# Turning the input of gate and up by transposing transfers for two of four batches

## The chip, the cores and the metric

The kernel runs on one core of one Trainium2 chip. The metric is the device time of one execution in microseconds (us). The core has five engines that run their own instruction queues and wait for each other through semaphores: TensorE (PE; its weight loads are shown as PEld), VectorE (DVE), ScalarE (ACT), GpSimd (POOL) and SyncE (SP), which here does nothing but start transfers. Each engine takes its instructions strictly in the order in which the program lists them.

## The reference

Four batches of 512 tokens, width 512, in single precision. Cut to what matters:

```python
x = _layernorm(x + attention(x, Wqkv, bqkv, Wo, bo))        # 16 heads
x = _layernorm(x + wkv(w, u, k=x, v=ctx))                   # a scan over the tokens
g = einsum('bsh,ih->bsi', x, (gate_w - 128) * gate_scale)   # 2048 wide
u = einsum('bsh,ih->bsi', x, (up_w - 128) * up_scale)
x = _layernorm(x + einsum('bsi,hi->bsh', silu(g) * u, (down_w - 128) * down_scale))
```

The second layernorm's output, called x2 below, is the input of gate and up. It stands in the tile `X[b]` with a token on each partition. The matmuls of gate and up sum over the 512 hidden columns, so they need x2 with a hidden column on each partition: it has to be turned.

## The kernel before

Numbers in single precision are multiplied as two 16-bit halves, a high one and a low one. For x2 these are `x2h` and `x2l`, each `[128, 2, 4, 512]`: 128 hidden columns, a slot of batch `b % 2`, four chunks c of hidden columns, 512 tokens.

The program's order is made by a timetable (`timetable()`): one list of pieces, with a slot counter, that every engine walks in the same order, each taking the pieces that are its own. Slots 0 to 275 are the attention of all four batches (16 head groups n of four heads, 16 slots a group). From slot 1000 (`FF`) on come gate, up and the down matmul, 20 slots a batch: 16 for the inner blocks `it`, then one for each `y(b, t)` (down, for 128 tokens t). Eight inner blocks of batch 0 (`EARLY`) are already spread over slots 246 to 276.

Turning x2 before the change, for each batch b and chunk c:

- piece `x2t`: PE transposes four 128x128 blocks of `X[b]` into one PSUM bank (`flip`, L1120, single precision);
- piece `x2h`: ACT reads the bank, scales by 64 and writes the high half in 16 bits (`x2_high`, L1359);
- piece `x2l`: DVE reads the bank again and writes what the high half lacks (`x2_low`, L1645).

`X2_AT` puts the four chunks of batch 0 at slots 222, 225, 226 and 233, and those of batch 1 all at slot 1018, which is after `y(0, 2)`. In the attention stage units like `x2t`, `wo`, `sv`, `pv` and `spread` share three PSUM banks. Batches 2 and 3 (`SEVEN`) use another scheme (`xf`, `xhi`, `xlo`) that the change leaves alone.

`gate_up` (L1133) waits for all of `x2h`, `x2l` of its batch. `y` is L1182 and L1184 (32 matmuls a piece). Around slot 1018 the list reads: `y(0, 1)`, `x1t(2, 2)`, `ek(2, 2)`, `scan_q(2, 2)`, `norm` and `out(0, 0)`, `scan_p`, `seed`, `refine(2, 2)`, `y(0, 2)` with its `yd`, `r3`, `rstd`, then `x2t(1, 0..3)`, `x1t(2, 3)`, `x2h` and `x2l` of batch 1, `ek(2, 3)`, `out(0, 1)`, further pieces of the scan, `y(0, 3)`, `gate(1, 0)`. `seed` (L1339, L1341) is an ACT piece of the scan and needs what POOL wrote at L1905.

SP starts, in this stretch of the attention, the transfers of `put` (L2057, the halves of q and k to memory), of `stack` (L2024, L2027, 128 KB each back into SBUF) and of `mput` (L2031 the shifts of a head group to memory, L2035 twice from there into `qs`); the transposed scores of group 14 (`turn`, L1056, first at slot 243) wait for the `mput(14)` at slot 238.

Of the kernel before, what the change touches and what calls it, by code (L numbers as in the profile page):

```python
# [5 lines left out]
ALU = mybir.AluOpType  # L6
ACT = mybir.ActivationFunctionType
# [5 lines left out]
P = 128  # L13
# [42 lines left out]
SEVEN = (2, 3)  # L56
PAIRS = IT // 2

SIGNAL = {"snap1": "snap", "snap5": "snap", "snap6": "snap", "c11": "summed", "c12": "summed", "c22": "summed"}

PART_READ = {1: 1, 2: 0, 3: 0, 4: 3, 5: 1, 6: 2, 7: 2}

# [29 lines left out]
            216, 15: 223}  # L92

WAIT = {'high': 1, 'low': 1, 'vtake': 2, 'r1': 2, 'norm': 6, 'exp': 4, 'eb': 0, 't1': 1, 't3': 0, 'oh': 2, 'ol':
        2, 'ek': 1, 'scan_q': 2, 'scan_p': 12, 'seed': 6, 'refine': 8, 'divide': 13, 'r2': 1, 'x2h': 0, 'x2l': 0,
        'expand': 0}
WAIT_IN = {'r1': 1, 'norm': 3, 'ek': 0, 'scan_q': 0, 'scan_p': 9, 'seed': 10, 'refine': 3, 'divide': 6, 'r2': 0,
           'x2h': 0, 'x2l': 0, 'norm2': 7}
PIECE_AT = {'load_second': 31, 'small': 66, 'split_wo': 47, 'load_ds': 180}
WU_AT = (44, 47, 48, 50)  # L100
WU_ZERO = (61, 119, 123, 144)
# [10 lines left out]
          3): 1040}  # L112
YT_AT = {0: (172, 178, 185, 191), 1: (1013, 1014, 1015, 1016), 2: (1026, 1027, 1028, 1029), 3: (1045, 1046, 1047,
         1049)}
X2_AT = {0: (222, 225, 226, 233), 1: (1018, 1018, 1018, 1018), 2: (1036, 1036, 1037, 1037), 3: (1057, 1057, 1057,
         1057)}
WO_IN = (7, 8, 9, 13)
WD_AT = (257, 257, 258, 261)
# [25 lines left out]
class Timetable:  # L144
# [45 lines left out]
def early(b, it):  # L190
# [11 lines left out]
    "bvo": lambda: ("bo",),  # L202
    "x1t": lambda b, c: ("ek", b, c),
    "yt": lambda b, t: ("r2", b, t),
    "x2t": lambda b, c: ("xf" if b in SEVEN else "x2l", b, c),
    "sa": lambda b, m: ("hfa", b, 2 * m + 1),
    "sb": lambda b, m: ("c11", b, m),
    "sd": lambda b, m: ("c12", b, m),
# [10 lines left out]
def timetable():  # L219
# [152 lines left out]

    def x2t(b, c):
        tt.flush(("norm", 1, b, 0, T))
        tt.unit("x2t", b, c)
        add("x2t", b, c)
        if b in SEVEN:
            late(wait("x2h"), lambda: quarters(b, c))
            return
        late(wait("x2h"), lambda: add("x2h", b, c))  # L380
        late(wait("x2l"), lambda: add("x2l", b, c))

    def quarters(b, c):
        add("xf", b, c)
# [8 lines left out]
    def gu_parts(b, it, pools):  # L393
        def part(p):
            name = "gate" if p < 2 else "up"
            if it == 0 and p == 0:
                tt.flush(("x2l", b, T - 1))
            if p % 2 == 0:
                tt.unit(name, b, it, pool=pools[p // 2])
                tt.unfinished.add((name, b, it))  # L400
            add(name, b, it, p % 2)
            if p % 2:
                tt.unfinished.discard((name, b, it))
            if p == 1:
                add("th", b, it)
                if early(b, it):
                    add("aa", b, it)
            if p == 3:
                add("hf", b, it)
# [287 lines left out]
def build(nc, ctx, xT, x, ctxT, wqkv, bqk, bv, wo, bo, wcol, ucol, gateT, gsc, upT, usc, downT, dsc,  # L697
# [47 lines left out]
    with ExitStack() as f:  # L745
# [10 lines left out]
        YS = sb(f, "ys", [P, 2, D], F32)  # L756
        S1A, S1B, S2B = (sb(f, n, [P, I], F16) for n in ("s1a", "s1b", "s2b"))
    CTS = [CT, CT, CT2, CT]
    RINGS = [(RING01[:, 0, :], RING01[:, 1, :]), (RING01[:, 2, :], RING01[:, 3, :]), (RING2[:, 0, :], RING2[:, 1, :])]


# [175 lines left out]
    def weight_sum(e, q, j, kk):  # L937
        a, c, op = {1: (wu[:, kk, :], wu[:, 2 + kk, :], ALU.add), 2: (WSUM[1][kk], wg[:, kk, :], ALU.subtract),
                    3: (wg[:, kk, :], wu[:, kk, :], ALU.subtract),
                    4: (wg[:, 2 + kk, :], WSUM[2][kk], ALU.subtract)}[j]  # L940
        q.wait_ge(*by("wo", B - 1, T - 1))
        if j == 4:
            q.wait_ge(sem("out0"), 16 * T)
        if j in (2, 4):
            q.wait_ge(*by_ws(j // 2, kk))
        e.tensor_tensor(WSUM[j][kk], a, c, op).then_inc(sem(f"ws{j}"), 1)
# [27 lines left out]
    def _(e):  # L974
# [148 lines left out]
        def gate_up(name, b, it, half):  # L1123
            bk, wt, s = bank[name, b, it], wg if name == "gate" else wu, b % 2
            if half == 0:
                emptied((name, b, it))
                pe.wait_ge(*by("x2h", b, T - 1))
                pe.wait_ge(*by("x2l", b, T - 1))
                pe.wait_ge(*by_zero("wg", T - 1))
                pe.wait_ge(*by_zero("wu", T - 1))  # L1130
            for k in (2 * half, 2 * half + 1):
                for xt in (x2h, x2l):
                    mm = e.matmul(PSB[:, bk, :], wt[:, k, it * P:(it + 1) * P], xt[:, s, k, :],  # L1133
                                  start=(k == 0 and xt is x2h), stop=(k == T - 1 and xt is x2l))
            if half:
                mm.then_inc(sem(name), 1)
# [104 lines left out]
    def _(e):  # L1241
# [104 lines left out]
            e.activation(X[b][:, t, :], X[b][:, t, :], ACT.Identity, bias=SHIFT[:, j:j + 1],  # L1346
                         scale=RS[:, 8 + b, t:t + 1]).then_inc(sem("norm2"), 1)

        def x2_high(b, c):
            act.wait_ge(*by("x2t", b, c))  # L1350
            if b >= 2:
                act.wait_ge(*by("up", b - 2, IT - 1))
            if b == 0:
                act.wait_ge(*by("qk", NG - 1, "k"))
                act.wait_ge(*by("v", B - 1, T - 1))
            elif b == 1:
                act.wait_ge(*by_put(NG - 1, "q"))
                act.wait_ge(*by_put(NG - 1, "k"))
            e.activation(x2h[:, b % 2, c, :], PSB[:, bank["x2t", b, c], :], ACT.Copy, scale=WS).then_inc(sem("x2h"), 1)  # L1359

        def x_full(b, c):
            act.wait_ge(*by("x2t", b, c))
# [143 lines left out]
    def _(e):  # L1506
# [132 lines left out]
            dve.wait_ge(sem(f"{name}_in{k * T // dst.shape[1]}"), 16)  # L1639
            e.tensor_scalar(dst[:, k, :], dst[:, k, :], -128.0, None, ALU.add).then_inc(sem("zero_" + name), 1)  # L1640

        def x2_low(b, c):
            s = b % 2
            dve.wait_ge(*by("x2h", b, c))
            e.scalar_tensor_tensor(out=x2l[:, s, c, :], in0=PSB[:, bank["x2t", b, c], :], scalar=WS, in1=x2h[:, s, c, :],  # L1645
                                   op0=ALU.mult, op1=ALU.subtract).then_inc(sem("x2l"), 1)

        def aa(b, it):
# [60 lines left out]
        def r3(b, t):  # L1709
            j = b * T + t  # L1710
            dve.wait_ge(*by("yd", b, t))
            dve.wait_ge(*by("x2t", b, T - 1))
            e.tensor_tensor(X[b][:, t, :], YS[:, j % 2, :], X[b][:, t, :], ALU.add).then_inc(sem("r3"), 1)
            stats(2, b, t, "r3")

# [15 lines left out]
        for name, *a in tt.order:  # L1731
# [8 lines left out]
                e.bn_aggr(MV[:, 2 * B + B - 1, T - 1, :], ST4[:]).then_inc(sem("ba2"), 1)  # L1740
            elif name == "scale_bqk":
                dve.wait_ge(sem("bqk"), 16)
                e.tensor_scalar(BQK[:], BQK[:], WS, None, ALU.mult).then_inc(sem("scale_bqk"), 1)
            elif name == "low":
                low(*a)
            elif name == "weigh":
# [11 lines left out]
            elif name == "bo":  # L1758
                dve.wait_ge(*by("bvo"))
                dve.wait_ge(*by_consts2())  # L1760
                e.tensor_tensor(BO[:], PSB[:, bank["bvo",], :], BO[:], ALU.add).then_inc(sem("bo"), 1)
            elif name == "split_wo":
                dve.wait_ge(sem("woh"), 1)
                dve.wait_ge(sem("warm"), 1)
# [235 lines left out]
    def _(e):  # L2000
# [37 lines left out]
        for name, *a in tt.order:  # L2038
# [11 lines left out]
            elif name == "load_w":  # L2050
                load_w(*a)
            elif name == "load_x":
                load_x(*a)
            elif name == "put":
                n, kind = a
                sp.wait_ge(*by("low", n, kind))
                e.dma_start(SCR[n, "qk".index(kind)].rearrange("l f t -> f l t"),  # L2057
                            HILO[kind][:]).then_inc(sem(f"put{kind}"), 16)
            elif name == "stack":
                stack(*a)  # L2060
            elif name == "mput":
# [86 lines left out]
```

## Time and profile before

| what | value |
|---|---|
| time, median of 3 runs | 710.17 us (708.37 to 712.4) |
| span of the profiled execution, first to last instruction | 709.9 us |
| busy: PE, DVE, ACT, POOL | 671.4, 513.2, 496.1, 395.7 us |
| mean clock granted to PE, of full speed | 0.989 |
| share of PE's pieces in the chain that ended last | 61% |

The profiled execution is one execution under the profiler. Its span lies 0.27 us below the median of the runs, inside their spread of 4 us. Every instruction has a start and a duration; where an engine stood idle before it, the trace names the instruction that ended the wait. A matmul's duration includes its passage through the array, so matmuls that follow each other overlap: what one costs in a row of many is the distance between their starts. "L1120" is a line of the kernel. The granted clock of PE is 1.00 at 2.4 GHz and 0.50 at 1.2 GHz.

### The profile page before, as it was taken

What the parts mean: (1) busy time and instruction counts of PE and PEld (TensorE: products, weight loads), DVE (VectorE), ACT (ScalarE), POOL (GpSimd) and SP (SyncE); (2) the same over time, 40 slices, a digit from 0 to 9 for tenths busy, and PEclk for the clock granted to TensorE, in tenths of its full rate; (3) what the DMA queues carried; (4) which work ended last, traced back from release to release, by engine and by line L of the source; (5) the groups of instructions that cost most, each with busy time, mean ns of one, the idle gap of its engine ahead of it and who ended that gap; (6) DMA issues with size and microseconds to landing.
All of it is one profiled execution on the core that took longest, in us unless ns stands there. A gap on an engine that the chain in (4) does not pass through costs nothing.

```text
span 709.9 us, 12525 instructions
## 1 busy us (share of the span) xinstructions
PE 671.4 (95%) x4290; PEld 380.8 (54%) x4290; DVE 513.2 (72%) x1220; ACT 496.1 (70%) x1143; POOL 395.7 (56%) x508
## 2 busy tenths in 40 slices
PE   8979999899988989799989999999999999999996
PEld 3435555445445545454445454544456797578845
DVE  4676767787888899989755569858777786655644
ACT  5798889789897879978787873384754855336620
POOL 6035735846999664864596654885771634103321
PEclk9999999999999999989999999999999999999999
DMA  7878944322332136460071002000001000000001
GB/s 239 249 218 235 217 145 135 98 75 79 124 102 78 38 85 163 120 143 16 8 120 60 1 0 75 16 31 0 1 1 44 17 1 2 30 31 1 1 16 45
DMA packets 45024, 54.33 MB, mean 77 GB/s; under 512 B 5921, under 2 KB 33825, under 8 KB 44961
## 3 DMA queue, kind: packets, MB, share of 16 engines
q1 hardware_dynamic: 41264, 46.85, 21.6%
q0 software_dynamic: 3264, 6.29, 5.4%
q8 instruction: 34, 0.56, 0.3%
q10 hardware_dynamic: 432, 0.39, 0.2%
q14 instruction: 30, 0.24, 0.1%
HBM read 45.00 MB, written 12.71 MB: 81 GB/s over the span
## 4 chain that ended last, share of the span: by engine, by line
PE 61%; DVE 13%; ACT 10%; POOL 5%; issue 5%; DMA 4%; SPq 1%; POOLq 0%; DVEq 0%; ACTq 0%
PE psb L1160 12%; PE psb L1133 8%; PE psb L996 6%; PE psb L1184 5%; PE psb L1182 5%; PE psb L1104 4%; PE psb L1072 4%; PE psb L1027 4%; DVE ee L1530 3%; PE psb L1039 3%; PE psb L1056 3%; DVE x L1607 2%; PE psb L1120 2%; PE psb L1083 2%; ACT L1330 1%
## 5 line engine op out<-in xcount | busy, mean ns | idle before, releaser
L1530 DVE CUSTOM_DVE_ANT_0 ee<-psb,mask,clip 128x512 f32<-128x512 f32 (+3 forms) x256 | 131.3, 542 | 24.9 <-PE psb L1039 22.3
L1278 ACT ACTIVATE ee<-ee,nm 128x512 f32<-128x512 f32 (+3 forms) x256 | 142.2, 560 | 1.4 <-DVE nm L1530 1.4
L1938 POOL TENSOR_TENSOR hl<-ring,hh 128x512 f16<-128x512 f32 x64 | 80.1, 1264 | 86.7 <-ACT hh L1414 57.3
L1288 ACT ACTIVATE ee<-psb 128x256 f32<-128x256 f32 (+1 forms) x192 | 94.6, 523 | 31.0 <-PE psb L1056 21.0
L1182 PE MATMUL psb<-wd,hh 128*128 128x512 f16 x240 | 91.0, 379 | 0.0
L1184 PE MATMUL psb<-wd,hl 128*128 128x512 f16 x240 | 91.0, 379 | 0.0
L1868 POOL TENSOR_SCALAR_AFFINE_SELECT ee<-ee 128x256 f32<-128x256 f32 x128 | 56.8, 452 | 60.7 <-ACT ee L1288 59.9
L1039 PE MATMUL psb<-ks,qs 128*128 128x512 f16 (+3 forms) x256 | 72.5, 305 | 8.3 <-DVE nm L1530 6.1
L1056 PE MATMUL psb<-qs,ks 128*128 128x128 f16 (+3 forms) x256 | 60.1, 306 | 9.6 <-ACT ee L1288 7.5
L996 PE MATMUL psb<-xh,wqk 128*128 128x512 f16 x240 | 61.8, 385 | 1.7 <-POOL xh L1830 1.2
L1885 POOL TENSOR_TENSOR rs<-ve,half 128x1 f32<-128x1 f32 (+1 forms) x24 | 20.5, 854 | 72.0 <-DVE ve L1599 71.7
L1278 ACT ACTIVATION_READ_ACCUMULATOR ee<-ee,nm 128x1 f32 x256 | 51.0, 199 | 0.0
L1133 PE MATMUL psb<-x2h,wg 128*128 128x512 f16 x128 | 48.6, 380 | 0.8 <-ACT ring L1426 0.5
L1133 PE MATMUL psb<-x2h,wu 128*128 128x512 f16 x128 | 48.5, 379 | 0.0
L1133 PE MATMUL psb<-x2l,wu 128*128 128x512 f16 x128 | 48.5, 379 | 0.0
L1133 PE MATMUL psb<-x2l,wg 128*128 128x512 f16 x128 | 48.5, 379 | 0.0
L1039 PEld LDWEIGHTS psb<-ks,qs 128*128 128x128 f16 x256 | 25.0, 99 | 35.6 <-DVE nm L1530 11.5
L1441 ACT ACTIVATE hh<-ring 128x512 bf16<-128x512 f32 x32 | 20.2, 630 | 30.6 <-DVE ring L1662 30.6
L1056 PEld LDWEIGHTS psb<-qs,ks 128*128 128x128 f16 x256 | 23.6, 99 | 32.1 <-ACT ee L1288 14.8
L1072 PE MATMUL psb<-ee,v 128*32 128x128 f32 (+3 forms) x512 | 37.8, 435 | 0.7 <-POOL ee L1868 0.6
L1184 PEld LDWEIGHTS psb<-wd,hl 128*128 128x128 f16 x240 | 23.4, 98 | 27.3 <-POOL hl L1938 0.2
L1182 PEld LDWEIGHTS psb<-wd,hh 128*128 128x128 bf16 x240 | 23.4, 98 | 27.2
(217 smaller groups left out, 1668.2 us busy)
## 6 DMA issues: line engine op xcount, KB each, us to landing
qs<-parts SPq DMA_DIRECT2D x48, 128.0 KB, 2.7
ks<-parts SPq DMA_DIRECT2D x45, 128.0 KB, 2.9
parts<-qhl SPq DMA_DIRECT2D x16, 256.0 KB, 2.2
parts<-khl SPq DMA_DIRECT2D x16, 256.0 KB, 2.2
x<-in_x SPq DMA_DIRECT2D x4, 1024.0 KB, 6.8
ct<-in_ctxT SPq DMA_DIRECT2D x4, 1024.0 KB, 5.1
out<-x SPq DMA_DIRECT2D x16, 256.0 KB, 2.0
xt<-in_xT SPq DMA_DIRECT2D x14, 256.0 KB, 3.4
```

Of the source, the lines that this page charges most:

```text
L996: mm = e.matmul(PSB[:, bk, :], wt[:, k, c0:c0 + P], xt[:, k, :], start=(p == 0 and k == 0), stop=(p == 2 and k == T - 1))
L1039: e.matmul(PSB[:, bank["score", H, i], 0:w], heads(n, "q")[:, h, i * P:(i + 1) * P], heads(n, "k")[:, h, 0:w], start=True, stop=True).then ...
L1056: mm = e.matmul(PSB[:, bk, o:o + (T - j) * P], heads(n, "k")[:, h, j * P:(j + 1) * P], heads(n, "q")[:, h, j * P:S], start=True, stop=True)
L1072: mm = e.matmul(PSB[32 * h:32 * h + 32, bk, j * P:S], VV[:, b % 2, j, g * P + 32 * h:g * P + 32 * h + 32], ET[(4 * n + h) % ET_SLOTS][:, T ...
L1133: mm = e.matmul(PSB[:, bk, :], wt[:, k, it * P:(it + 1) * P], xt[:, s, k, :], start=(k == 0 and xt is x2h), stop=(k == T - 1 and xt is x2l))
L1160: mm = e.matmul(PSB[:, bk, k * HALF_S:(k + 1) * HALF_S], weights(j, kk, 2 * m + k), moving(b, j, kk, low), start=(unit is not None and k + ...
L1182: e.matmul(PSB[:, bk, :], HS[it][0][:, t * P:(t + 1) * P], wd[:, it, :], start=(it == 0), stop=False)
L1184: mm = e.matmul(PSB[:, bk, :], HS[it][1][:, t * P:(t + 1) * P], wd[:, it, :], start=False, stop=(it == IT - 1))
L1278: e.activation(dst, dst, ACT.Exp, bias=NM[:, n % 4, col:col + 1], scale=-1.0, accum_out=DEN[:, n % 4, col:col + 1]).then_inc(sem("exp"), 1)
L1288: e.activation(ET[H % ET_SLOTS][:, base:base + width], PSB[:, bank["turn", H, item], 0:width], ACT.Exp, scale=SC).then_inc(sem("et"), 1)
L1530: e.tensor_tensor_reduce(E[H % E_SLOTS][:, EOFF[i]:EOFF[i] + w], PSB[:, bank["score", H, i], 0:w], MASK[:, S - w:S], -SC, CLIP[:, i:i + 1] ...
L1938: e.tensor_tensor(HS[it][1][:], pair(b, it // 2)[:, it % 2, :] if b in SEVEN else ring(b, it)[1], HS[it][0][:], ALU.subtract).then_inc(sem ...
```

## The change

For batches 0 and 1 the three pieces change their order: first the split, by token, then the turn, by transfers.

- `x2h`: ACT reads `X[b][:, t, :]` (SBUF, tokens t) and writes the high half into a staging tile `STAGED[b][0]`, still with a token on each partition. `x2l`: DVE does the same for the low half, from SBUF too.
- `xtr`, new, on SP: for each t, two transposing transfers of `[128 tokens, 512]` in 16 bits (128 KB each), from the staging tiles into `x2h` and `x2l`. That is 8 a batch, 16 in all. Each set waits for its `x2l`.
- `x2t` is gone for these batches: 8 pieces, 32 PE transposes.
- Batch 0 stages in the slot of batch 1 of `x2h`, `x2l`; batch 1 stages in `S1B`, `S2B`, which are weight sums of the later scheme, so `weight_sum` with j 1 or 2 and kk 1 now waits for batch 1's transfers. The staging tile of batch 0 overlaps the halves of q and k, so `x2l` of batch 0 waits for `put(15)`.
- `X2_AT[0]` moves from (222, 225, 226, 233) to (231, 231, 232, 232). Batch 1 stays at slot 1018.
- `gate_up` waits for the transfers (`by_turned_x2`). `r3` waits for `x2h` where it waited for `x2t`. Two semaphores of other pieces (`scale_bqk`, `bo`) become one.

```diff
-X2_AT = {0: (222, 225, 226, 233), 1: (1018, 1018, 1018, 1018), ...
+X2_AT = {0: (231, 231, 232, 232), 1: (1018, 1018, 1018, 1018), ...
...
     def x2t(b, c):
         tt.flush(("norm", 1, b, 0, T))
+        if b not in SEVEN:
+            for name in ("x2h", "x2l", "xtr"):
+                add(name, b, c)
+            return
...
+    STAGED = [(x2h[:, 1, :, :], x2l[:, 1, :, :]), tuple(w[:].rearrange("p (t n) -> p t n", t=T) for w in (S1B, S2B))]
...
+    def by_turned_x2(b):
+        return sem("xtr"), 2 * 16 * T * (b + 1)
...
+        if j in (1, 2) and kk == 1:
+            q.wait_ge(*by_turned_x2(1))
...
-                pe.wait_ge(*by("x2h", b, T - 1))
-                pe.wait_ge(*by("x2l", b, T - 1))
+                pe.wait_ge(*by_turned_x2(b))
...
-        def x2_high(b, c):
-            act.wait_ge(*by("x2t", b, c))
...
+        def x2_high(b, t):
+            act.wait_ge(*by_norm(1, b, t))
+            if b:
+                act.wait_ge(*by("wo", B - 1, T - 1))
+            else:
                 act.wait_ge(*by("qk", NG - 1, "k"))
                 act.wait_ge(*by("v", B - 1, T - 1))
...
-            e.activation(x2h[:, b % 2, c, :], PSB[:, bank["x2t", b, c], :], ACT.Copy, scale=WS).then_inc(sem("x2h"), 1)
+            e.activation(STAGED[b][0][:, t, :], X[b][:, t, :], ACT.Copy, scale=WS).then_inc(sem("x2h"), 1)
...
+        def x2_low(b, t):
+            dve.wait_ge(*by("x2h", b, t))
+            if b == 0:
+                dve.wait_ge(*by_put(NG - 1, "q"))
+                dve.wait_ge(*by_put(NG - 1, "k"))
+            e.scalar_tensor_tensor(out=STAGED[b][1][:, t, :], in0=X[b][:, t, :], scalar=WS, in1=STAGED[b][0][:, t, :],
                                    op0=ALU.mult, op1=ALU.subtract).then_inc(sem("x2l"), 1)
...
+            elif name == "xtr":
+                b, t = a
+                sp.wait_ge(*by("x2l", b, t))
+                if b:
+                    sp.wait_ge(*by_turned_x2(b - 1))
+                for k, to in enumerate((x2h, x2l)):
+                    e.dma_start_transpose(to[:, b, :, t * P:(t + 1) * P], STAGED[b][k][:, t, :]).then_inc(sem("xtr"), 16)
```

## Rows read from the trace of the kernel before

**Rows 1.** Busy time of the engines in stretches (first line: the columns).
```profile
core 0: us, PE busy (x) PEld busy (x) DVE busy (x) ACT busy (x) POOL busy (x), PEclk, DMA share, GB/s
320.00:330.00 10.00, 9.56 (x73) 4.97 (x66) 9.41 (x28) 8.26 (x27) 4.56 (x9) 1.00 0.01 3
455.00:520.00 65.00, 64.32 (x310) 30.46 (x309) 46.70 (x59) 41.47 (x57) 47.28 (x39) 1.00 0.03 13
```

**Rows 2.** Timeline, PE, batch 0's transposes: start, us, engine, line, tiles, count.
```profile
308.30 0.86 PE L1120 MATMUL psb<-ident,x 128*128 128x128 f32 x4
309.00 0.22 PE L1039 MATMUL psb<-ks,qs 128*128 128x128 f16 x1
...
312.59 0.60 PE L1120 MATMUL psb<-ident,x 128*128 128x128 f32 x4
313.03 0.27 PE L1039 MATMUL psb<-ks,qs 128*128 128x256 f16 x1
```

**Rows 3.** Timeline, 305 to 314 us: waits around batch 0's first chunk.
```profile
309.83 0.69 DVE L1645 SCALAR_TENSOR_TENSOR x2l<-psb,x2h 128x512 f16<-128x512 f32 x1 [2.32 <-ACT x2h L1359]
310.57 1.16 PE L1083 MATMUL psb<-lt,v 128*128 128x128 f32 x8 [0.26 <-DVE x2l L1645]
```

**Rows 4.** Timeline, DVE, where slots 231 and 232 fall.
```profile
320.31 0.35 DVE L1530 CUSTOM_DVE_ANT_0 ee<-psb,mask,clip 128x128 f32<-128x128 f32 x1
322.71 0.74 DVE L1530 CUSTOM_DVE_ANT_0 ee<-psb,mask,clip 128x512 f32<-128x512 f32 x1
```

**Rows 5.** Timeline, SP and PE: the shifts of group 14 and their first reader.
```profile
328.47 0.31 SPq L2031 DMA_DIRECT2D shifts<-mrow  x1
329.84 0.78 SPq L2035 DMA_DIRECT2D qs<-shifts  x2
332.76 0.49 PE L1056 MATMUL psb<-qs,ks 128*128 128x512 f16 x2
```

**Rows 6.** Timeline around slot 1018, all engines.
```profile
445.88 2.32 PEld L1120 LDWEIGHTS psb<-ident,x 128*128 128x128 f32 x20
448.17 0.10 PEld L1182 LDWEIGHTS psb<-wd,hh 128*128 128x128 bf16 x1
...
450.90 0.63 ACT L1339 ACTIVATE qs_<-ek 128x512 f32<-128x512 f32 x1 [9.55 <-POOL ek L1905]
452.11 2.04 ACT L1359 ACTIVATE x2h<-psb 128x512 f16<-128x512 f32 x4
452.72 2.48 DVE L1645 SCALAR_TENSOR_TENSOR x2l<-psb,x2h 128x512 f16<-128x512 f32 x4 [1.83 <-ACT x2h L1359]
...
455.35 0.38 PE L1133 MATMUL psb<-x2h,wg 128*128 128x512 f16 x1
```

**Rows 7.** Lines of SP: ns to issue one (min/median/max), and us to landing.
```profile
L2027 SPq DMA_DIRECT2D ks<-parts x45: 303/432/1152, 24.5 to 315.2; - x45
...
DMA to landing us min/median/max: 2.4/2.8/7.6
...
L2035 SPq DMA_DIRECT2D qs<-shifts x32: 302/372/1726, 38.2 to 352.5; - x32
...
DMA to landing us min/median/max: 2.1/2.2/4.4
...
L2049 SPq DMA_DIRECT2D ident<-in_cmask x1: 2146/2146/2146, 5.8 to 5.8; - x1
```

**Rows 8.** Stretches before and at a fall of PE's clock (columns as in Rows 1).
```profile
298.40:301.00 2.60, 0.40 (x3) 0.10 (x1) 2.60 (x4) 2.38 (x7) 1.36 (x2) 1.00 1.04 170
302.00:308.80 6.80, 6.10 (x19) 2.47 (x17) 5.28 (x13) 3.75 (x10) 6.70 (x9) 0.50 0.26 68
216.70:220.10 3.40, 3.40 (x16) 2.88 (x15) 2.04 (x10) 2.78 (x9) 3.25 (x5) 0.50 0.14 46
```

**Rows 9.** By line and shape, whole span: the low half from PSUM, and one from SBUF.
```profile
L1645 DVE SCALAR_TENSOR_TENSOR x2l<-psb,x2h 128x512 f16<-128x512 f32 x8 | 5.2, 685 | 4.6 <-ACT x2h L1359 4.6
L1766 DVE SCALAR_TENSOR_TENSOR wol<-ct,woh 128x512 f16<-128x512 f32 x4 | 2.5, 694 | 1.5 <-ACT woh L1476 1.5
```

More of the change, by code:

```diff
@@ L57 @@
 PAIRS = IT // 2
-SIGNAL = {"snap1": "snap", "snap5": "snap", "snap6": "snap", "c11": "summed", "c12": "summed", "c22": "summed"}
+SIGNAL = {"snap1": "snap", "snap5": "snap", "snap6": "snap", "c11": "summed", "c12": "summed", "c22": "summed", "scale_bqk": "biases", "bo": "biases"}
 PART_READ = {1: 1, 2: 0, 3: 0, 4: 3, 5: 1, 6: 2, 7: 2}
@@ L94 @@
 WAIT = {'high': 1, 'low': 1, 'vtake': 2, 'r1': 2, 'norm': 6, 'exp': 4, 'eb': 0, 't1': 1, 't3': 0, 'oh': 2, 'ol':
-        2, 'ek': 1, 'scan_q': 2, 'scan_p': 12, 'seed': 6, 'refine': 8, 'divide': 13, 'r2': 1, 'x2h': 0, 'x2l': 0,
+        2, 'ek': 1, 'scan_q': 2, 'scan_p': 12, 'seed': 6, 'refine': 8, 'divide': 13, 'r2': 1, 'x2h': 0,
         'expand': 0}
 WAIT_IN = {'r1': 1, 'norm': 3, 'ek': 0, 'scan_q': 0, 'scan_p': 9, 'seed': 10, 'refine': 3, 'divide': 6, 'r2': 0,
-           'x2h': 0, 'x2l': 0, 'norm2': 7}
+           'x2h': 0, 'norm2': 7}
 PIECE_AT = {'load_second': 31, 'small': 66, 'split_wo': 47, 'load_ds': 180}
@@ L114 @@
          1049)}
-X2_AT = {0: (222, 225, 226, 233), 1: (1018, 1018, 1018, 1018), 2: (1036, 1036, 1037, 1037), 3: (1057, 1057, 1057,
+X2_AT = {0: (231, 231, 232, 232), 1: (1018, 1018, 1018, 1018), 2: (1036, 1036, 1037, 1037), 3: (1057, 1057, 1057,
          1057)}
@@ L204 @@
     "yt": lambda b, t: ("r2", b, t),
-    "x2t": lambda b, c: ("xf" if b in SEVEN else "x2l", b, c),
+    "x2t": lambda b, c: ("xf", b, c),
     "sa": lambda b, m: ("hfa", b, 2 * m + 1),
@@ L374, in x2t @@
         tt.flush(("norm", 1, b, 0, T))
+        if b not in SEVEN:
+            for name in ("x2h", "x2l", "xtr"):
+                add(name, b, c)
+            return
         tt.unit("x2t", b, c)
         add("x2t", b, c)
[L377 to L381, printed above, removed]
+        late(wait("x2h"), lambda: quarters(b, c))
     def quarters(b, c):
@@ L396, in part @@
             if it == 0 and p == 0:
-                tt.flush(("x2l", b, T - 1))
+                tt.flush(("xtr", b, T - 1))
             if p % 2 == 0:
@@ L1347, in out_norm @@
                          scale=RS[:, 8 + b, t:t + 1]).then_inc(sem("norm2"), 1)
-        def x2_high(b, c):
-            act.wait_ge(*by("x2t", b, c))
-            if b >= 2:
-                act.wait_ge(*by("up", b - 2, IT - 1))
-            if b == 0:
+        def x2_high(b, t):
[3 more added lines that the diff above has]
+            else:
                 act.wait_ge(*by("qk", NG - 1, "k"))
                 act.wait_ge(*by("v", B - 1, T - 1))
-            elif b == 1:
-                act.wait_ge(*by_put(NG - 1, "q"))
-                act.wait_ge(*by_put(NG - 1, "k"))
-            e.activation(x2h[:, b % 2, c, :], PSB[:, bank["x2t", b, c], :], ACT.Copy, scale=WS).then_inc(sem("x2h"), 1)
+            e.activation(STAGED[b][0][:, t, :], X[b][:, t, :], ACT.Copy, scale=WS).then_inc(sem("x2h"), 1)
         def x_full(b, c):
@@ L1640, in zero @@
             e.tensor_scalar(dst[:, k, :], dst[:, k, :], -128.0, None, ALU.add).then_inc(sem("zero_" + name), 1)
[L1642 to L1645, printed above, removed]
+        def x2_low(b, t):
[4 more added lines that the diff above has]
+            e.scalar_tensor_tensor(out=STAGED[b][1][:, t, :], in0=X[b][:, t, :], scalar=WS, in1=STAGED[b][0][:, t, :],
                                    op0=ALU.mult, op1=ALU.subtract).then_inc(sem("x2l"), 1)
@@ L1711, in r3 @@
             dve.wait_ge(*by("yd", b, t))
-            dve.wait_ge(*by("x2t", b, T - 1))
+            dve.wait_ge(*by("x2t" if b in SEVEN else "x2h", b, T - 1))
             e.tensor_tensor(X[b][:, t, :], YS[:, j % 2, :], X[b][:, t, :], ALU.add).then_inc(sem("r3"), 1)
@@ L1742, in _ @@
                 dve.wait_ge(sem("bqk"), 16)
-                e.tensor_scalar(BQK[:], BQK[:], WS, None, ALU.mult).then_inc(sem("scale_bqk"), 1)
+                e.tensor_scalar(BQK[:], BQK[:], WS, None, ALU.mult).then_inc(sem("biases"), 1)
             elif name == "low":
@@ L1760, in _ @@
                 dve.wait_ge(*by_consts2())
-                e.tensor_tensor(BO[:], PSB[:, bank["bvo",], :], BO[:], ALU.add).then_inc(sem("bo"), 1)
+                e.tensor_tensor(BO[:], PSB[:, bank["bvo",], :], BO[:], ALU.add).then_inc(sem("biases"), 1)
             elif name == "split_wo":
```

## The prediction

> **What bounds the kernel now.** I read the busy time of the engines by stretches first [rows 1]. Behind the attention PE is the bound: 64.32 of 65.0 us, no other engine over 47.3. What PE loses there is lost for good; what it is spared is gained only if nothing else is late. In the attention two engines are close: of 10 us around slot 231 PE is busy 9.56 and DVE 9.41. The change meets both kinds of stretch: batch 0 in the attention, batch 1 at the seam between the down matmul of batch 0 and gate and up of batch 1. So I read the timelines of those two places next, engine by engine, and asked of each: which wait ends last before the first matmul that reads x2?
>
> At the seam the answer is plain [rows 6]. PE ends `y(0, 2)`, does 20 transposes in 2.32 us (16 of batch 1's x2, 4 for the scan), then `y(0, 3)` from 448.17, and the first gate matmul of batch 1 starts at 455.35. The last of the four `x2l` ends at 452.72 + 2.48 = 455.20. So the gate starts as soon as `x2l` is there: the seam has no slack at all. Nor is `x2l` late because of PE's transposes. ACT sat idle for 9.55 us until POOL's L1905 let the scan's `seed` go at 450.90, and `x2h` stands behind that `seed` in ACT's queue, so it began at 452.11, four microseconds after its banks were full. The change leaves `seed` ahead of `x2h`: both are added where they were.
>
> **Part 1, PE is spared 32 transposes.** In batch 0 a chunk of four costs the distance to the next start: 0.70 us for the first, which ran at the low clock, and 0.44 for the second [rows 2]; the other two cost about as much as the second, so 0.70 + 3 x 0.44 = 2.0 us. With them goes a wait of PE for the bank, 0.26, and one of DVE for `x2h`, 2.32 [rows 3]. DVE is nearly as full as PE, so its idle time counts too, but it lies beside PE's 0.70 of the same chunk and isn't added twice. I take 2.0 + 0.3 = 2.3 us gained, with ends 0 (DVE remains the bound) and 2.8. In batch 1 PE is spared 2.32 x 16/20 = 1.86 us, but that gains nothing, since `x2l` is what the gate waits for: `y(0, 3)` now ends at about 453.3 in the clock of before, and PE waits.
>
> **Part 2, the split from SBUF.** Eight pieces on ACT and eight on DVE as before, with another source. DVE's `x2l` from PSUM takes 685 ns, the same operation from SBUF (L1766) 694 [rows 9]. ACT's I leave at the 2.04 us that four took [rows 6]. Nothing, either way. Four `x2l` now stand in two slots instead of four; the 2.8 us of DVE work is the same, only bunched, and PE has matmuls of the out projection to go on with. Nothing, at most 0.7 (one `x2l` in front of a score that PE waits for).
>
> **Part 3, batch 1's turn.** This is new work on the path that sets the end. From each `x2l` on: two transfers to issue by SP, in order, then the landing of the eighth, then the gate. Nothing else of SP stands in the way; behind it waits only an output that nobody reads on the chip. The DMA engines are idle (share 0.03 on average after 455) [rows 1].
>
> The trace of before holds no transposing transfer. Its cost is bounded by the nearest rows [rows 7]. Lower end: `ks<-parts`, 128 KB into SBUF by the same queue, takes SP 0.43 us to issue (median). Upper end: the longest issue I found, 2.15. Landing after issue begins: 2.4 to 7.6 us, median 2.8. I take 1.0 us for an issue, near the longest that a transfer of this very size took (1.15), because eight follow each other and each is cut finer than one that keeps its rows; and 2.8 for landing.
>
> The first `x2l` ends at 452.72 + 0.69 = 453.4. The eighth issue begins 7 x 1.0 later, at 460.4, and lands at 463.2. Against 455.35 the gate is late by **7.9 us**. With 0.43 and 2.4 it would be 458.8, late by 3.5; with 2.15 and 2.8 it would be 471.3, late by 15.9.
>
> **Part 4, PE's clock.** PE then stands idle from 453.3 to 463.2. In the trace a stretch of 2.60 us in which PE worked 0.40 was followed by 6.8 us at 1.2 GHz; another fall lasted 3.4 us [rows 8]. Half the length is lost while PE has work: 1.7 to 3.4 us. I take **1.7**, with 0 as the lower end, since a fall may pass while PE is idle anyway.
>
> **Part 5, batch 0's turn.** DVE comes to `x2l` of slot 231 behind the score at 320.31, so the first ends at about 321.4 and the second at 322.0; the other two stand behind the score at 322.71 and end near 325.5 and 326.2 [rows 4]. At 1.0 us an issue SP is done with eight at about 329.5. The gate of batch 0 comes at slot 246, some ten slots after that, so its own wait is covered. What isn't, is SP's queue: `mput(14)` is next in it. Before, it was issued at 328.47, the second of its two reads was begun at 330.2 (329.84 and one issue of 0.37) and landed 2.2 us later, at 332.4, and the transposed score that reads it started at 332.76 [rows 5, 7]. The cover is 0.35 us. SP would come to it 1.0 us later: PE loses **0.7**. At 0.43 an issue: nothing. At 2.15: eight end at 338.6, ten late, PE loses 9.8.
>
> **Part 6, the rest.** The merged semaphore counts the same two pieces in the same order; `r3` waits for a piece long done; `weight_sum`'s new wait falls some blocks into gate and up of batch 1, tens of microseconds after the eighth landing, in front of nothing that PE wants at once. POOL's queue is not touched. All nothing.
>
> **The sum.** +7.9 + 1.7 + 0.7 - 2.3 = +8.0 us against the profiled execution (span 709.9). The median of the runs is 0.3 above that span, within their spread, so I add to it: 710.2 + 8.0 = **718.2 us**, 1.1% slower.
>
> **Rivals.** (A) *An issue costs what any other of its size costs.* Place: SP's queue at the seam; price 3.5 to 3.9 late, minus 2.3, plus 0 to 1.7: +1.2 to +3.3, 712.4 in the middle, which is no change by the measure. For it speaks that every 128 KB row lies near 0.43; against it, that no row turns anything. It decides below 0.47 us an issue, where the sum -1.95 + 7 x issue + 2.8 + 1.7 - 2.3 falls under 3.55 us (0.5%). It can't well become faster: with no fall of the clock and 2.8 gained it is still +0.7, as two transfers must come after an `x2l` that was itself just in time.
> The Trainium skill (Advanced Engine Details and Errata, section X-Bar Transpose (TRN2)) has the rule that speaks for A: transposing transfers are as fast as regular ones. No row of before shows one; by that rule 712.4.
>
> (C) *They are served one after the other, each when the last has landed.* Eight times 2.8 is 22.4: the gate at 475.8, late by 20.4, plus a fall of 3.4, minus 2.3: +21.5, 732. If the shifts of group 14 stand behind batch 0's eight in the same rings (321.4 + 22.4 = 343.8, plus the 3.9 that they take, against 332.76) PE loses another 15: 747. Against it: an ordinary transfer's issue of 0.43 beside a landing of 2.8 [rows 7] means that several are under way at once.
> PE's own price is 2.32/20 = 0.12 us a square in a row of twenty [rows 6]. The Trainium skill (VectorE: DVE Perf Modes, section The three transpose paths) speaks against the change here: 1309 ns for one 128x128 square by the DMA crossbar, 390 by TensorE; the row has TensorE at a third of that, and the crossbar in no row. By the Trainium skill's figure four squares take 5.2 us and eight transfers 42, an estimate of some +40 us.
>
> **How the numbers follow.** Forecast (issue 0.6 to 1.3 us): 50%, own range 712 to 726 (0.6: 460.0, +4.7, no fall, -2.8; 1.3: 465.3, +10.0, +3.4, -1, +3.0 for the shifts). Rival A: 26%, 710.5 to 713.5. Rival C: 14%, 732 to 747. Between forecast and C: 5%. Faster for a reason that I don't see, such as the fall of 6.8 us at 302 being gone in most runs together with A: 5%. The range **710.5 to 731** leaves out C, and the faster cases: about 2 in 10. A measurement of this kernel tells 0.5% (3.6 us) from no change: faster 0.05, same 0.28 (A and the lower edge of the forecast), slower 0.67.
>
> **What would show it.** In the changed kernel's timeline: `x2h` of batch 1 still right behind the scan's `seed` on ACT; a gap on PE behind `y(0, 3)` that ends with the transposing transfers, of 5 (A), 10 (forecast) or over 20 us (C); a granted clock of 0.50 right after it; SP's rows of the new line show the issue (0.43, 1.0 or more) and the landing; `mput(14)` issued after the eighth. Wrong would be: no gap of PE there, `x2h` of batch 1 well ahead of `seed`, or PE waiting longest in the attention instead.

## The result: 1.7% slower

| | before | after |
|---|---|---|
| time, median of 4 runs each | 711.28 us (708.37 to 713.31) | 721.84 us (720.86 to 724.86) |
| ratio, 95% interval | | 1.0174, 1.0132 to 1.0216 |
| span of the profiled execution | 709.9 us | 720.9 us |

The waits of PE over the whole span of after name the two places at once. The columns are: who waited for what, us in total, times, longest.

```profile
PE psb L1138 <- DMA x2l<-s2b: 12.1, 1, 12.1
...
PE psb L1062 <- DMA qs<-shifts: 3.4, 2, 2.9
```

The first is the seam, where L1138 is the gate of batch 1; the second is the transposed score of group 14. Next the timeline of the seam in after, which answers to [rows 6].

```profile
451.28 0.63 ACT L1344 ACTIVATE qs_<-ek 128x512 f32<-128x512 f32 x1 [9.56 <-POOL ek L1909]
...
452.48 2.17 ACT L1361 ACTIVATE s1b<-x 128x512 f16<-128x512 f32 x4
...
453.13 3.87 DVE L1649 SCALAR_TENSOR_TENSOR s2b<-x,s1b 128x512 f16<-128x512 f32 x4 [1.87 <-ACT s1b L1361]
...
454.32 1.20 SPq L2095 DMA_TRANSPOSE x2h<-s1b  x1
455.56 1.27 SPq L2095 DMA_TRANSPOSE x2l<-s2b  x1
...
463.41 1.27 SPq L2095 DMA_TRANSPOSE x2l<-s2b  x1
...
466.04 0.59 PE L1138 MATMUL psb<-x2h,wg 128*128 128x512 f16 x1 [12.07 <-DMA x2l<-s2b]
```

`seed` (L1344) still waits for POOL and `x2h` stands right behind it. Eight issues follow each other without a pause, 1.24 us from the first to the second and 1.31 between most of the others (454.32 to 463.41 is 9.09 us for 7 distances), and PE stands idle for 12.07 us. The issues and the landing by line (ns to issue, shortest, median, longest; then us from issue to landing):

```profile
L2095 SPq DMA_TRANSPOSE x2h<-s1b x4: 1196/1264/1265, 454.3 to 462.1; - x4
L2095 SPq DMA_TRANSPOSE x2l<-s2b x4: 1267/1267/1267, 455.6 to 463.4; - x4
...
DMA to landing us min/median/max: 2.4/2.5/4.2
```

Stretches of after, columns as in [rows 1]: the gap, and the fall of the clock that begins in it and ends 3.1 us after the gate has started.

```profile
453.70:466.00 12.30, 0.27 (x2) 0.00 (x0) 11.73 (x13) 6.06 (x9) 10.72 (x10) 0.71 0.44 91
459.00:469.30 10.30, 3.26 (x9) 1.23 (x10) 7.12 (x8) 3.25 (x4) 7.00 (x7) 0.51 0.45 116
```

Two traces are compared here by the start of the same matmul in each. The clock falls elsewhere too, and not at the same places in each execution (before: 6.8 us at 302, [rows 8]; after: none there), so a shift is read only across the stretch in question, and even there a fall in one of the two traces has to be taken out. Up to `y(0, 2)` after is 0.37 us behind before. The gate of batch 1 starts 10.69 us behind (455.35 and 466.04), so the seam costs **10.32**. Eight matmuls at half clock add 1.51 (12.20). Between 480 and 486 us 1.25 of that is regained, where before had small waits of its own: after is then 10.95 behind, and stays so to the end.

Batch 0, timeline of SP, ACT and PE in after, which answers to [rows 5]:

```profile
317.85 2.21 SPq L2095 DMA_TRANSPOSE x2h<-x2h  x1
...
327.96 1.27 SPq L2095 DMA_TRANSPOSE x2l<-x2l  x1
329.28 0.58 SPq L2035 DMA_DIRECT2D shifts<-mrow  x1
330.90 0.77 SPq L2039 DMA_DIRECT2D qs<-shifts  x2
...
325.40 0.27 ACT L1300 ACTIVATE mrow<-psb 32x128 f16<-32x128 f32 x1
...
333.50 0.27 PE L1062 MATMUL psb<-qs,ks 128*128 128x256 f16 x1 [2.88 <-DMA qs<-shifts]
```

The rows to be moved are there at 325.67, but the shifts (L2035) are issued at 329.28, behind the eighth transfer.

### The profile page after: what moved, and what is told of

The parts are those of the page before. It is cut to its first block, busy times and chain, and to the rows that moved or that the text cites. A ratio compares the mean times of both kernels' runs of the same rounds, so it can differ in the third digit from the quotient of the medians.

```text
span 720.9 us, 12476 instructions
## 1 busy us (share of the span) xinstructions
PE 667.5 (93%) x4258; PEld 377.7 (52%) x4258; DVE 516.3 (72%) x1220; ACT 497.6 (69%) x1143; POOL 396.1 (55%) x508
## 4 chain that ended last, share of the span: by engine, by line
PE 61%; DVE 12%; ACT 9%; DMA 5%; issue 5%; POOL 4%; SPq 3%; POOLq 0%; DVEq 0%; ACTq 0%
PE psb L1165 12%; PE psb L1138 12%; PE psb L1002 5%; PE psb L1187 5%; PE psb L1189 5%; PE psb L1033 4%; PE psb L1110 4%; PE psb L1078 4%; DVE ee L1532 3%; PE psb L1062 3%; PE psb L1045 3%; DVE x L1609 2%; SPq L2095 2%; PE psb L1126 2%; ACT ee L1283 2%
## 5 line engine op out<-in xcount | busy, mean ns | idle before, releaser
L1138 PE MATMUL psb<-x2h,wg 128*128 128x512 f16 x128 | 49.5, 387 | 12.2 <-DMA x2l<-s2b 12.1
L1138 PE MATMUL psb<-x2l,wg 128*128 128x512 f16 x128 | 49.4, 386 | 0.0
L1138 PE MATMUL psb<-x2h,wu 128*128 128x512 f16 x128 | 48.5, 379 | 0.0
L1138 PE MATMUL psb<-x2l,wu 128*128 128x512 f16 x128 | 48.5, 379 | 0.0
L1666 DVE SCALAR_TENSOR_TENSOR ring<-ring,c,psb 128x512 f32<-128x512 f32 x24 | 17.9, 747 | 33.8 <-ACT ring L1428 22.3
```

## The experiments

Theory T: nearly all of the loss is batch 1's turn at the seam, the issues of SP behind a late `x2l`; batch 0 comes out about even. Its rivals: batch 0 carries much of it (R1), or any transfer there costs as much, turned or not (R2). Each time is set against executions of before on the same chip. The table gives what the traces say about the seam, worked out as above: when the gate of batch 1 starts, how far the kernel is from before ahead of the seam, and what the seam has cost by the start of the gate and by the last down matmul.

| kernel | gate (1, 0) | ahead | cost at the gate | cost at the end |
|---|---|---|---|---|
| after | 466.04 | +0.37 | +10.32 | +10.58 |
| batch 0 alone | 455.28 | -0.09 | +0.03 | +0.02 |
| batch 1 alone | 464.09 | -1.70 | +10.44 | +11.64 |
| shifts first | 461.34 | -4.35 | +10.34 | +10.47 |
| plain copies | 460.29 | -1.09 | +6.03 | +6.16 |
| split early | 462.33 | +5.04 | +1.95 | +2.39 |
| half turned | 466.75 | +1.39 | +10.02 | +11.61 |
| filler | 466.99 | +0.90 | +10.74 | +9.50 |
| joined | 459.45 | -2.08 | +6.18 | +6.41 |
| joined, early | 450.66 | -2.77 | -1.92 | +1.95 |

The last two columns differ by the fall of the clock behind the gap less what is regained later. The fall is not the same in each execution: 1.51 us in after, 2.44 in batch 1 alone, 2.83 in half turned; regained are 1.24 or 1.25 in all three. A gate "in the clock of after" below is the gate less the "ahead" of its own row, plus 0.37.

**One batch at a time.** The edit: `b in (0,)` or `b in (1,)` takes the new path, the other batch keeps `x2t`, `x2h`, `x2l` at the old slots.

> Only batch 0 is split and turned by transfers; batch 1 goes over PE as before. Theory T (the loss is batch 1's turn at the seam, eight issues of 1.3 us in SP's queue behind x2l): what PE is spared in batch 0 (2.3 us) and what it loses in waiting for the shifts of group 14 (about 2.9) cancel, so 0 to +1 us against before, about 711 to 712; the seam is as before, the first gate matmul of batch 1 right behind the fourth x2l. Rival R1 (batch 0 carries a good part, by the shifts' wait and the bunched x2l): +4 us or more.

> Only batch 1 is split and turned by transfers; batch 0 goes over PE at its old slots. Theory T: about +10.5 us, about 721.8, as after; the PE gap behind y(0, 3) ends with the transposing transfers and is as long as in after, followed by the clock at 0.50. Rival R1 (batch 0 carries a good part): +7 us or less.

Measured: batch 0 alone 711.92 against 710.06 us, ratio 1.0022 (0.9997 to 1.0048). Batch 1 alone 720.70, ratio 1.0153 (1.0100 to 1.0206), +10.6 us. The gate of batch 1 in batch 0 alone, then in batch 1 alone:

```profile
455.28 0.38 PE L1145 MATMUL psb<-x2h,wg 128*128 128x512 f16 x1
```
```profile
464.09 0.58 PE L1147 MATMUL psb<-x2h,wg 128*128 128x512 f16 x1 [12.20 <-DMA x2l<-s2b]
```

R1 falls. Batch 0 alone is near the upper edge of what T said, or a little over it.

Since both kernels have the same seam or the same batch 0 as after, batch 0's own parts can be read off too. Against batch 1 alone, the transposed scores of after shift by -2.40 us between 298 and 322 us (-2.42 in batch 0 alone), by +1.04 from there to 326 us, and by +2.44 at the shifts of group 14: +1.08 in all.

The -2.40 has three parts. Batch 1 alone ran 3.4 us at half clock here, where after and batch 0 alone had no fall (a stretch of batch 1 alone, columns as in [rows 1]):

```profile
301.50:305.30 3.80, 3.38 (x10) 1.04 (x9) 3.73 (x8) 3.10 (x8) 3.72 (x6) 0.55 0.23 73
```

That is 0.57 us of the shift, and none of it comes from the change. PE's transposes and its wait for the bank are 2.27. Against them stands a wait that grew by 0.44 at the first score behind the bunched split (batch 1 alone, then after):

```profile
322.02 0.28 PE L1067 MATMUL psb<-qs,ks 128*128 128x256 f16 x1 [0.25 <-ACT ee L1302]
```
```profile
320.62 0.28 PE L1062 MATMUL psb<-qs,ks 128*128 128x256 f16 x1 [0.69 <-ACT ee L1293]
```

So the change gains 2.27 here and loses 0.44 + 1.04 = 1.48 around the split.

**The shifts first.** Two of batch 0's four pieces `xtr` are listed behind `mput(14)`:

```diff
     def shifts(n):
         ...
         add("mput", n)
+        if n == NG - 2:
+            add("xtr", 0, 2)
+            add("xtr", 0, 3)
```

> Both batches by transfers, but four of batch 0's eight transposing transfers stand behind the shifts of group 14 in SP's list instead of ahead of them. Theory T: the wait of 2.9 us of the transposed score on qs<-shifts falls under 0.5, and the time by 2 to 3 us against after, to about 719; the gate of batch 0, some ten slots later, doesn't wait for the transfers. Rival (DVE is as full as PE there, so PE's wait only moves to DVE's tiles): the wait falls, and the time stays at that of after, 721.8.

SP's timeline in that kernel, and PE's wait over its whole span:

```profile
320.62 1.28 SPq L2100 DMA_TRANSPOSE x2l<-x2l  x1
324.01 0.33 SPq L2040 DMA_DIRECT2D shifts<-mrow  x1
```
```profile
PE psb L1067 <- DMA qs<-shifts: 1.0, 1, 1.0
```

The shifts go out at once, and of the wait 1.0 us is left in the whole span, none of it between 315 and 334. From 298 us to batch 0's gate this kernel loses nothing against batch 1 alone but gains 1.90, where after loses 1.08: a gain of 3.0 in that stretch, and none of it is the clock's, since this kernel had a fall there and after had none. Its time doesn't show it: 721.39 us (717.78 to 724.23), ratio 1.0161 (1.0107 to 1.0214), too wide to tell it from after. The kernels with batch 0 alone, below, tell it better.

**Plain copies.** `dma_start` in place of `dma_start_transpose`, the same pieces and bytes.

> All sixteen transposing transfers are ordinary transfers of the same pieces; left out is the turn itself, so x2h and x2l of batches 0 and 1 hold tokens where hidden columns should be. Theory T (the turning form costs 1.27 us of SP's time an issue, an ordinary transfer of this size 0.43): SP keeps up with x2l, the gate of batch 1 starts at the last x2l (457.0 in the clock of after) + 0.4 + 2.4, about 460 against 466, and the time is 715 to 716. Rival R2 (a transfer as such is what costs, turned or not): the gate at about 466 as in after, 721 to 722.

Measured 715.60 us, ratio 1.0073 (1.0047 to 1.0099). R2 falls as it was put, though more than half of the loss at the gate, 6.03 of 10.32 us, stays. By line, and the gate:

```profile
L2095 SPq DMA_DIRECT2D x2h<-s1b x4: 594/623/654, 452.9 to 457.1; - x4
L2095 SPq DMA_DIRECT2D x2l<-s2b x4: 639/644/650, 453.5 to 457.8; - x4
...
DMA to landing us min/median/max: 2.3/2.4/4.0
```
```profile
460.29 0.58 PE L1138 MATMUL psb<-x2h,wg 128*128 128x512 f16 x1 [7.78 <-DMA x2l<-s2b]
```

So 4.3 of the 10.3 us (10.32 - 6.03) are the turning form, nearly all of it in the issue: 1.27 us against 0.64, and 4.89 from the first issue to the eighth against 9.09. Landing is the same. The other 6.0 are 0.55 by which the first transfer goes out later than the first `x2l` ended in before, these 4.89, and 2.53 to the gate, less the 1.94 that before itself has from its first `x2l` to the gate. An issue of 0.43, which T took from [rows 7], isn't reached with these pieces either, and SP did not keep up with `x2l`. T's 460 was meant in the clock of after, where this gate comes at 461.75, 1.7 later; that it stands at 460.29 in its own trace is chance.

**Split early.** `X2_AT[1]` is 1017 in place of 1018, so `x2h` stands ahead of `seed` on ACT; the last piece that subtracts 128 from the down weights (`ZERO_IN`) moves one slot earlier with it.

> As after, with batch 1's split and turn one slot earlier (1017 in place of 1018), so that its x2h stands ahead of the scan's seed on ACT and not behind it. Theory T (the loss is what lies between a late x2l and the gate, and x2l is late because of the place behind seed): x2l begins right behind the second layernorm of batch 1, near 443.5 us in the clock of after, eight issues of 1.31 us end near 455, the gate comes at 457 to 458 instead of 466, eight us earlier, the clock falls less, and the time is 712 to 715. Rival (the scan behind x2h and x2l becomes late in their place and gives the gain back): the gate comes early, but the time stays above 718.

Measured 714.77 us, ratio 1.0067 (1.0041 to 1.0092). The profiled execution was the slowest of the eight.

```profile
449.92 2.49 DVE L1649 SCALAR_TENSOR_TENSOR s2b<-x,s1b 128x512 f16<-128x512 f32 x4
```
```profile
462.33 0.49 PE L1138 MATMUL psb<-x2h,wg 128*128 128x512 f16 x1 [3.70 <-DMA x2l<-s2b]
```

The seam costs 1.95 in place of 10.32: the place of the split is worth 8.4 us. In the clock of after the gate comes at 457.7, as expected. The four `x2l` take 2.49 again.

**Half turned.** Batch 1's transfers turn two chunks of four.

```diff
+n = T // (1 + b)
...
-e.dma_start_transpose(to[:, b, :, t * P:(t + 1) * P], STAGED[b][k][:, t, :]).then_inc(sem("xtr"), 16)
+e.dma_start_transpose(to[:, b, 0:n, t * P:(t + 1) * P], STAGED[b][k][:, t, 0:n * P]).then_inc(sem("xtr"), 16)
```

> Batch 1's eight transposing transfers turn two of the four chunks each (64 KB in place of 128 KB); left out is the turn of chunks 2 and 3 of batch 1, so those parts of x2h and x2l hold old numbers. If the price goes by the 128x128 squares, an issue takes 0.6 to 0.8 us in place of 1.27 and the gate comes 2.5 to 4 us earlier than in after (from 466.0, to 462 or 463), limited by x2l, whose fourth ends at 457. If it goes by the transfer, the issue stays at 1.2 to 1.3 us and the gate at 466.

```profile
L2096 SPq DMA_TRANSPOSE x2h<-s1b x4: 1175/1244/1244, 455.3 to 463.0; - x4
L2096 SPq DMA_TRANSPOSE x2l<-s2b x4: 1246/1247/1247, 456.5 to 464.3; - x4
...
DMA to landing us min/median/max: 2.3/2.4/5.3
```

Half the bytes, the same issue (1.25) and a seam of +10.02. From 64 to 128 KB the price goes by the transfer. This is read from the trace; the kernel ran once, in 724.68 us.

**Filler.** PE does 56 spare matmuls ahead of the gate's wait.

```diff
+if (name, b, it) == ("gate", 1, 0):
+    for _ in range(FILL):   # 56
+        e.matmul(PSB[:, bk, :], wd[:, 0, 0:P], wd[:, 1, :], start=True, stop=True)
```

> As after, with 56 more matmuls of 128x512 on loaded weights between y(0, 3) and the gate of batch 1 on PE, into the bank that the gate then overwrites: some 12 us of work that fills the gap. Theory T (PE's idle gap makes the clock fall, and that costs 1.5 us of its own): no stretch at 0.50 behind the gap, the gate at the same time as in after, and the time 1 to 2 us below after's, near 720. Rival (the fall costs nothing, since PE waits for others later anyway): no stretch at 0.50 either, but later waits of PE grow by the same and the time stays at 721 to 722.

```profile
466.99 0.39 PE L1142 MATMUL psb<-x2h,wg 128*128 128x512 f16 x1 [0.40 <-DMA x2l<-s2b]
467.21 0.38 PE L1142 MATMUL psb<-x2l,wg 128*128 128x512 f16 x1
```

The gate's matmuls follow at 0.22 us, the granted clock has no stretch at 0.50 there, and the seam costs 9.50 by the end in place of 10.58. The rival, that later waits grow by as much, falls in the trace: 1.24 is regained later, as in after. So the fall costs 1.5 us, of which 1.1 shows at the end, because the gate came 0.4 later here; the first issue took 1.99 us in place of 1.20:

```profile
454.57 1.99 SPq L2099 DMA_TRANSPOSE x2h<-s1b  x1
```

The runs, 722.20 us and 1.0167 (1.0133 to 1.0200), can't tell 1 us; the trace bears T out, the time leaves it open.

**Joined.** High and low half of 128 tokens lie side by side in one staging tile and one tile `X2`, and are turned by one transfer of 256 KB: four in place of eight for batch 1.

```diff
+e.dma_start_transpose(X2[:, b, :, :, t * P:(t + 1) * P].rearrange("p j c n -> p (j c) n"),
+                      JOINED[:, t, :, :].rearrange("p j n -> p (j n)")).then_inc(sem("xtr"), 16)
```

> As after, with batch 1's transfers joined: the high and the low half of 128 tokens stand side by side in the staging tile and are turned by one transfer of 256 KB, so four transfers in place of eight, in the same place behind x2l, with the same bytes. If the price goes by the transfer (theory T after the run that turned half as much at the same 1.25 us an issue): issue 1.2 to 1.35 us each, SP keeps up with x2l, the fourth lands near 461 to 462 in place of 465.9 (clock of after), and the time is 3.5 to 5 us under after's, 717 to 718. If it goes by the bytes once they are above 128 KB: issue near 2.5 us each and the gate at 466, 721 to 722.

```profile
L2098 SPq DMA_TRANSPOSE x2both<-s x4: 1231/1282/1332, 451.9 to 456.0; - x4
...
DMA to landing us min/median/max: 3.1/3.2/3.4
```

Twice the bytes at the same issue, 0.7 us more to land. The seam costs 6.18, which is 4.1 less, and in the clock of after the gate comes at 461.9; both as expected. The time is 719.86 us (716.11 to 722.52), 1.0142 (1.0107 to 1.0177), lower than after but above what was expected; four scattered runs don't settle it to 2 us.

**Versions that might beat before.** Batch 0 alone with the shifts first, run twice; the same with its split in four slots in place of two; and batch 1 joined and early, with batch 0's shifts first.

> Only batch 0 by transfers, and four of its eight stand behind the shifts of group 14 in SP's list. Theory T (batch 0 gains what PE is spared, 2.3 us, less about 1.0 at the bunched x2l, once the shifts aren't behind the transfers): 0.7 to 2 us below before, ratio 0.997 to 0.999, and about 2.5 us below the kernel with batch 0 alone. Rival (DVE is the bound in that stretch and PE's spared time is not gained): the same as before or above it.

> The kernel with batch 0 alone and the shifts first once more, beside the spread one on the same chip: 708 to 709.5, ratio 0.996 to 0.999, if the gain seen first was no accident of the runs; 710 or above if it was.

> As the kernel with batch 0 alone and the shifts first, with batch 0's four pieces of the split in slots 230, 231, 232, 233 in place of two in 231 and two in 232. Theory T (the bunched x2l stand ahead of scores that PE's turned scores wait for; PE's waits there add up to about 1.5 us against 0.25 before): the step of +1.0 us between the shift of PE's turned scores at 318 and at 324 us halves or goes, and the time is 0.5 to 1 us under the bunched kernel, 707.5 to 708.5. Rival (DVE is as full as PE there, so the same 2.6 us of x2l cost the same wherever they stand): the step stays at 1.0, the time at 708.6.

> Batch 1's four joined transfers, its split one slot earlier (1017), and for batch 0 four of the eight transfers behind the shifts of group 14. Theory T: four issues of 1.3 us behind an x2l that ends some 6 us ahead of the end of y(0, 3) land before y(0, 3) ends, PE has no gap at the seam and gains the 1.86 us of transposes of batch 1, beside 1 to 2 us of batch 0: 3 to 4 us below before, 706 to 707, ratio 0.994 to 0.996. Rival (the place ahead of seed delays the scan of batch 2, and PE or DVE pay for it later): at 709 or above.

| kernel | time | before, same chip | ratio, 95% |
|---|---|---|---|
| batch 0, shifts first | 708.64 | 710.16 | 0.9970 (0.9946 to 0.9995) |
| the same again | 708.96 | 709.00 | 0.9988 (0.9964 to 1.0012) |
| batch 0, shifts first, split spread | 708.33 | 709.00 | 0.9978 (0.9956 to 0.9999) |
| batch 1 joined and early, shifts first | 710.09 | 710.24 | 1.0000 (0.9982 to 1.0018) |

Batch 0 with the shifts first gains 2.0 us in both traces, counted as above against batch 1 alone. Of this 0.6 is again the fall that only batch 1 alone had, so the change is worth 1.4; the intervals put it between no gain and 0.5%. Spreading the split gained 1.30 in its trace, not more, and the loss around the split is as large as with the bunched one (1.5 us in both): the theory that bunching causes it falls. What remains fits DVE being full there, 9.90 of the 10 us from 320 in after, where before had 9.41 [rows 1]; no run tests that by itself.

```profile
320.00:330.00 10.00, 8.58 (x48) 4.39 (x49) 9.90 (x32) 8.76 (x28) 5.93 (x13) 1.00 0.58 103
```

The last kernel, joined and early, is the one to learn from; its 706 to 707 us were missed, and the rival's 709 or more came. PE has no gap at the seam and gains 1.92 us there. Then it waits, and its clock falls (timeline, and a stretch with columns as in [rows 1]):

```profile
478.33 0.66 PE L1134 MATMUL psb<-ident,ct 128*128 128x128 f32 x4 [1.69 <-ACT ring L1436]
```
```profile
480.00:483.30 3.30, 3.30 (x10) 1.16 (x8) 2.41 (x3) 1.15 (x3) 1.35 (x2) 0.53 0.00 0
```

ACT's `ring` stands behind the next `seed` of the scan. It is 1.81 us earlier than in before (477.59 and 479.40) where PE is 4.69 earlier. From the start of the gate to the end 3.87 us are given back (-1.92 to +1.95 in the table). 2.88 of them go at this wait (-4.69 to -1.81): the 1.92 that PE had gained at the seam and the scan did not follow, and 0.96 by which the scan itself is late. The rest, 0.99, goes in the fall of the clock behind it, less what is regained. Split early tells where the 0.96 comes from, since it has the early split without the joined transfers. The first `seed` in split early, then here:

```profile
457.38 0.63 ACT L1344 ACTIVATE qs_<-ek 128x512 f32<-128x512 f32 x1 [7.13 <-POOL ek L1909]
```
```profile
449.58 0.63 ACT L1352 ACTIVATE qs_<-ek 128x512 f32<-128x512 f32 x1 [7.13 <-POOL ek L1917]
```

Against before's 450.90 [rows 6], and with what each kernel was ahead or behind taken out, that is 1.44 and 1.45 us late, and the `ring` is 0.95 and 0.96 late. With the split in its old place the same `seed` is within 0.03 of before, and 0.27 early in the filler's trace. So the early split does delay the scan.

## Why the prediction was right, and where its sizes were off

The sign, the place and the mechanism came out as forecast: `x2h` right behind `seed`, one gap of PE behind `y(0, 3)`, a low clock after it, `mput(14)` behind the eighth issue. The time, 721.84, lies inside the range and 3.6 us above the 718.2. That it came so near is in part luck: three terms were too small, all in the same direction, and 1.25 us regained later and a fall of the clock that after happened not to have hid some of it.

| term | forecast | measured |
|---|---|---|
| first `x2l` ends (first issue 454.32, less 0.37) | 453.4 | 453.9 |
| first to eighth issue | 7.0 | 9.1 |
| landing | 2.8 | 2.5 |
| gate of batch 1 late | 7.9 | 10.3 |
| half clock behind the gap | 1.7 | 1.5 |
| regained later | 0 | -1.25 |
| PE spared in batch 0 | -2.3 | -2.3 |
| half clock near 302 us, in batch 1 alone and not in after | - | -0.6 |
| split of batch 0 on DVE | 0 (to 0.7) | +1.5 |
| shifts of group 14 | 0.7 | +2.4 |
| sum | +8.0 | +11.7 |

The sum adds the gate and the six rows below it, before rounding. It stands beside 11.0 between the two spans, 10.6 between the two medians and +12.4 (9.4 to 15.4) from the ratio. The three larger misses:

- **Part 3, the issue.** It was put at 1.0 us between 0.43 and 2.15; it is 1.27, with 1.30 from one to the next on average. That is 2.1 us at the seam. The choice of a value above the plain transfers was right; the reason given, finer pieces, explains only 0.43 to 0.64, which plain copies of these pieces cost. The rest is the turning form, for which the prediction had no row, so that 1.0 came near 1.27 was luck.
- **Part 5, the shifts.** The same price: the prediction's own line said 3.0 at 1.3 us an issue. The 2.21 us of the first issue came on top. The step at the wait itself is 3.0; 0.6 of it is made up by waits of PE close by that were gone. The shifts first undid it.
- **Part 2, the split from SBUF.** "Nothing, either way" was wrong at both places. In batch 0 PE's waits for DVE and ACT grew. At the seam the price per piece was read from `wol` [rows 9], beside which POOL computed on nothing wider than 16 columns. Here four `x2l` took 3.87 us against 2.48 [rows 6]. Of this only the 0.5 by which the first one ends later is in the seam's 10.32: SP went from the first issue to the eighth without a pause, so that the fourth `x2l`, 1.4 later than in before, held up nothing.

Part 4 was right in size, but not that part of it would be regained. Part 1's 2.3 was right as a stretch, and the loss around the split, where DVE is nearly full, ate 1.5 of it.

Rival A said that an issue costs what any other costs. It does not: 1.27 against 0.43 [rows 7], and against 0.64 in plain copies of the same pieces. The rule of the Trainium skill (Advanced Engine Details and Errata, section X-Bar Transpose (TRN2)), that transposing transfers are as fast as regular ones, holds here for landing (2.5 and 2.4 us) and not for eight in a row. Rival C would have shown a distance of 2.8 from one issue to the next. The Trainium skill's 1309 ns for one 128x128 square (VectorE: DVE Perf Modes, section The three transpose paths) does not add up square by square here: 1.29, 1.31 and 1.27 to 1.38 us lie between whole transfers of two, four and eight squares, and no run turns one square alone. The eight transfers took 9.09 + 2.63 us from the first issue to the gate, where the prediction's estimate from that figure had 42.

## What to carry to other kernels

Work taken off a full engine is worth only what the replacement doesn't put on the path: here 1.9 us of transposes of batch 1 were traded for eight issues behind a split that was already just in time, and splitting earlier, with the same transfers, took away 8.4 of the 10.3 us. Read a transfer's price as issue times number plus one landing, ask what stands behind it in the same queue, and issue the short urgent ones first. When a gap is closed, follow the engine on: the next wait may be close behind, as in the kernel that closed the seam and lost all of it some 28 us later.

## What the hardware showed that was not expected

- A transposing transfer costs SP 1.25, 1.27 and 1.28 us to issue with 64, 128 and 256 KB; landing takes 2.4, 2.5 and 3.2 us. Joining two by two about halves the queue's time: 4.15 us from the first issue to the last in place of 9.09.
- `x2l` with both inputs in SBUF is slowed beside POOL. In after, at the seam, then `x2l` from PSUM in before at the same place, by tile (shortest, median, longest ns):

```profile
L1649 DVE SCALAR_TENSOR_TENSOR s2b<-x,s1b x4: 679/924/1575, 453.1 to 456.3; 128x512 f16<-128x512 f32 x4
```
```profile
L1645 DVE SCALAR_TENSOR_TENSOR x2l<-psb,x2h x4: 678/680/691, 452.7 to 454.5; 128x512 f16<-128x512 f32 x4
```

POOL ran its `[128, 512]` operations beside the first two pieces in after, and one of them took longer too:

```profile
452.65 1.09 POOL L1919 TENSOR_TENSOR ek<-ek,qs_ 128x512 f32<-128x512 f32 x1 [0.17 <-ACT qs_ L1346]
...
453.83 1.42 POOL L1922 TENSOR_TENSOR ct<-ct,qs_ 128x512 f32<-128x512 f32 x1
```

The 1.17 and 1.58 us of these two pieces stand in all seven kernels that split batch 1 late and turn it by transfers. With the split early, where POOL's tiles were `[128, 1]`, the four took 2.49, and batch 0's four in after, with no such POOL instruction beside them, 0.68 to 0.69 each. No run took POOL's work away alone, so the cause is read from these rows and not shown by an experiment. The Trainium skill (GPSIMD Engine Reference, section 1. Specifications) has the rule that GpSimd's way into SBUF is shared with VectorE and that a VectorE instruction with two SBUF inputs contends there; the rows agree with it.
